# Cross-attention and expert layer on one core: the PV products of a quad in three bursts of two key tiles in place of two bursts of three

## The chip, the cores and the metric

One core of a Trainium2 chip runs the whole program. The metric is the device time of one execution in microseconds; the number compared is the median over runs. TensorE is PE in the profile (its weight loads PEld), VectorE DVE, ScalarE ACT, GpSimd POOL, SyncE SP.

## The reference

For 8 batch entries of 256 tokens and 128 channels there is a cross-attention with 16 heads of 8 dimensions. The keys and values of a head are 512 context rows, given, and the 256 own rows, projected from the layer-normalised input. A mixture of 8 experts, two for each token, follows.

```
qkv  = layernorm(x) @ w_qkv.T                    # q, own k, own v
k, v = concat(context k, k), concat(context v, v)   # 512 + 256 = 768 keys
attn = softmax(q * scale @ k.T)
x    = x + (attn @ v) @ w_proj.T + b_proj
x    = x + sum over the 2 chosen experts of weight * down(silu(gate(h)) * up(h)),   h = layernorm(x)
```

The change touches only `attn @ v`, and there only the order of the work.

## The kernel before, in words

Two functions run one after the other: `attend` (all of the attention) and `experts`. Each engine has its own instruction list, written out by hand; semaphores tie the lists together. Nothing plans or reorders the work.

`attend` handles the heads in quads of G = 4. There are QUADS = 32 of them: 8 batch entries times T = 4 quads. Quad q belongs to batch entry q // 4. The 768 keys are KT = 6 key tiles of 128. The program steps s from -2 to 33; b and r are s // 4 and s % 4. In step s three quads are in flight:

- Quad s + 2 has its row maxima computed. TensorE makes scores for that in six units (`max_half`, lines 528 and 533, each unit in two halves) into two PSUM buffers of two banks, `max_ps`. VectorE reduces each unit (`reduce_unit`, line 433). Half units wait until the unit two before has been reduced.
- Quad s has its scores made again, transposed and with the maximum already subtracted, in 12 units (`exp_unit`, line 550; unit 2k + a is key tile k and head pair a) into two single banks, `exp_ps[a]`. ScalarE exponentiates each unit into `probs` (line 392). Unit u waits until ScalarE has finished unit u - 2.
- Quad s - 1, and quad s itself, have their probabilities multiplied with the values: `pv_tile(q, k)` (line 560) is key tile k of quad q, four matmuls of 128 keys by 32 columns, one for each head, all accumulated into the one bank `pv_ps`. It waits for units 2k and 2k + 1 of ScalarE, and its first tile for the copy of the bank of the quad before.

TensorE's list in a step is GROUPS = 6 groups. Group i is: max half of one half of the rows, exp unit 2i, max half of the other half, exp unit 2i + 1. They are ordered so that neighbours use different halves of the array's rows. Between the groups stand other matmuls on whole rows: before group 1 the output projection of the batch entry before (r = 1, line 580) or the key and query projection (r = 2, lines 510 and 511); before group 3 the transposed maxima of the next quad (line 541); before group 4 the transposed result of quad s - 1 (line 568); before group 5 the transposed attention (r = 0, line 574), the transposed input (r = 1, line 505) or the value projection (r = 2, line 516). Those at r = 1 and 2 stop near the end of the batch. After group 1 and after group 4 stand the bursts of `pv_tile`s that the change moves.

ScalarE's list in a step is the 12 units, with the copy of `pv_ps` to SBUF (line 381) ahead of unit 4, which waits for the last `pv_tile` of quad s - 1, and the copy of the transposed maxima (line 386) ahead of unit 6. VectorE's list is the six reductions, with the normalising of quad s - 1 (lines 447 and 451, which wait for the transposed result) behind the fourth, and the merged row maxima (line 440) at the end. GpSimd refills the value columns of a quad when its products are done (`fill_values`, line 270). SyncE's queue spreads the keys and queries of quad s + 4 once all scores of quad s have been made.

Of the kernel before, what the change touches and what calls it, by code (L numbers as in the profile page):

```python
# [34 lines left out]
KT = CT + QT  # L35
# [14 lines left out]
def wait_for(engine, sem, value):  # L50

    if not isinstance(value, int) or value > 0:
        engine.wait_ge(sem, value)
# [39 lines left out]
def attend(nc, m, d):  # L93
# [13 lines left out]
    with ExitStack() as ctx:  # L107
# [55 lines left out]
        has_scores = lambda s: 0 <= s < QUADS  # L163
# [337 lines left out]
        def _(pe):  # L501
            def transpose_x(c):
                pe.wait_ge(norm_out, QT * (c + 1))
                for q in range(QT):
                    mm = pe.transpose(shared_ps[:, q * P:(q + 1) * P], xn[:, QT * c + q, :], m.ident[:])
                mm.then_inc(xt_filled, 1)

            def project_keys_queries(c):
                pe.wait_ge(xt_copied, c + 1)
                pe.matmul(shared_ps[:, 0:N], wqkv[:, C:2 * C], xnT[:], start=True, stop=True)  # L510
                pe.matmul(shared_ps[:, N:2 * N], wqkv[:, 0:C], xnT[:], start=True, stop=True).then_inc(kq_filled, 1)

            def project_values(c):
                pe.wait_ge(kq_copied, 2 * c + 2)
                for q in range(QT):
                    mm = pe.matmul(shared_ps[:, q * C:(q + 1) * C], xnT[:, q * P:(q + 1) * P], wqkv[:, 2 * C:3 * C],
                                   start=True, stop=True)
                mm.then_inc(v_filled, 1)

            def max_half(q, w, a):  # L520
                t, rows = q % T, slice(TILE * a, TILE * (a + 1))
                if w == 0 and a:
                    pe.wait_ge(rows_in[t], rows_spread(q))
                if a:
                    wait_for(pe, max_done, q * MUNITS + w - 1)
                if w < G:
                    g, i = divmod(w, QT)
                    mm = pe.matmul(max_ps[w % 2][:, a * BANK:(a + 1) * BANK], blocks[rows, t, g, i * P:(i + 1) * P],  # L528
                                   keys[rows, t, 0:NC_], start=True, stop=True)
                else:  # L530
                    for i in range(QT):
                        first = a * BANK + i * N
                        mm = pe.matmul(max_ps[w % 2][:, first:first + N], blocks[rows, t, w - G, i * P:(i + 1) * P],  # L533
                                       keys[rows, t, NC_:KEYS], start=True, stop=True)
                if a == 0:
                    mm.then_inc(max_filled, 1)

            def transpose_maxima(q):
                pe.wait_ge(split_max, 2 * q + 2)
                for i in range(QT):  # L540
                    mm = pe.transpose(shared_r[:, i * P:(i + 1) * P], maxes[:, q % 2, i, :], ident_r[:])
                mm.then_inc(maxT_filled, 1)

            def exp_unit(q, u):
                t, (k, a) = q % T, divmod(u, 2)
                rows = slice(TILE * a, TILE * (a + 1))
                if u == 0:
                    pe.wait_ge(max_in[t], 16 * (q // T + 1))
                wait_for(pe, exp_done, q * XUNITS + u - 1)
                pe.matmul(exp_ps[a][:], keys[rows, t, k * P:(k + 1) * P], blocks[rows, t], start=True, stop=True)\  # L550
                  .then_inc(exp_filled, 1)

            def pv_tile(q, k):
                t = q % T
                if k == 0:
                    pe.wait_ge(values_ready, 2 * q + 2)
                    wait_for(pe, pv_copied, q)
                pe.wait_ge(exp_done, q * XUNITS + 2 * (k + 1))
                for g in range(G):
                    mm = pe.matmul(pv_ps[ROWS * g:ROWS * (g + 1), 0:N], value_cols[:, t, k, g, :],  # L560
                                   probs[q % 2][:, k, g, :], start=(k == 0), stop=(k == KT - 1))
                if k == KT - 1:
                    mm.then_inc(pv_filled, 1)

            def transpose_out(q):
                pe.wait_ge(pv_copied, q + 1)
                for i in range(QT):
                    mm = pe.transpose(shared_ps[:, i * P:(i + 1) * P], pv_sb[:, i * P:(i + 1) * P], m.ident[:])
                mm.then_inc(out_filled, 1)

            def transpose_attention(b):
                pe.wait_ge(out_done, T * (b + 1))
                for i in range(QT):
                    mm = pe.transpose(shared_ps[:, i * P:(i + 1) * P], attn[:, i, :], m.ident[:])
                mm.then_inc(attnT_filled, 1)

            def project_out(b):
                pe.wait_ge(attnT_copied, b + 1)
                for i in range(QT):
                    mm = pe.matmul(shared_ps[:, i * C:(i + 1) * C], attnT[:, i, :], wproj[:], start=True, stop=True)  # L580
                mm.then_inc(proj_filled, 1)
# [13 lines left out]
            def step(s, b, r):  # L595
                for i in range(GROUPS):
                    if i == 1:
                        if r == 1 and b >= 1:
                            project_out(b - 1)
                        if r == 2 and b + 2 < B:  # L600
                            project_keys_queries(b + 2)
                    if i == 3 and has_scores(s + 1):
                        wait_for(pe, out_done, s - 1)
                        if r == 1 and b >= 1:
                            pe.wait_ge(proj_done, b)
                        if r == 2 and b + 2 < B:
                            pe.wait_ge(kq_copied, 2 * (b + 2) + 2)
                        if r == 3 and b + 2 < B:
                            pe.wait_ge(v_copied, b + 3)
                        transpose_maxima(s + 1)  # L610
                    if i == 4 and 1 <= s <= QUADS:
                        if has_scores(s + 1):
                            pe.wait_ge(maxT_copied, s + 2)
                        else:
                            wait_for(pe, out_done, s - 1)
                        transpose_out(s - 1)
                    if i == 5:
                        if r == 0 and b >= 1:
                            transpose_attention(b - 1)
                        if r == 1 and 0 <= b < B - 2:  # L620
                            pe.wait_ge(out_done, s)
                            transpose_x(b + 2)
                        if r == 2 and b + 2 < B:
                            wait_for(pe, out_done, s)
                            project_values(b + 2)
                    for a in range(2):
                        if has_scores(s + 2):
                            max_half(s + 2, i, 1 - a)
                        if has_scores(s):
                            exp_unit(s, 2 * i + a)  # L630
                    if i == 1 and has_scores(s - 1):
                        for k in range(KT // 2, KT):
                            pv_tile(s - 1, k)
                    if i == 4 and has_scores(s):
                        for k in range(KT // 2):
                            pv_tile(s, k)

            steps(step)


# [488 lines left out]
```

## Time and profile before

| | us |
|---|---|
| median of 3 runs (lowest, highest) | 576.71 (576.43, 577.19) |
| time of the profiled execution | 573.06 |
| its span | 571.5 |
| PE busy | 486.9 (85%) |
| DVE busy | 354.5 (62%) |
| ACT busy | 293.8 (51%) |
| POOL busy | 180.5 (32%) |

The span is that of the instructions in the profiled execution. An engine is busy while an instruction of its kind runs; matmuls are pipelined, so PE busy counts overlapping ones once and does not mean PE at its peak. In the chain that ended last only 2% of the span is named by an engine's line. The attention takes the first 363 us or so, the experts the rest.

### The profile page before, as it was taken

To read this page: it belongs to the slowest core of one execution; us is meant where nothing else is said; L and a number is where in the kernel's file an instruction comes from. 1 tells how busy PE (TensorE), PEld (TensorE's weight loads), DVE (VectorE), ACT (ScalarE), POOL (GpSimd) and SP (SyncE) were. 2 spreads that over 40 slices of the span, in tenths; PEclk is the share of its full clock that TensorE was granted. 3 is DMA by queue.
4 is the path that set the end of the run, shared out by engine and by line. 5 is a ranking of instruction groups with operands and counts; after the bars stand their busy time and mean duration, and the time that the engine had idled before them with its cause. 6 is when DMAs were issued, how large, how long until landed. Compare 5 with 4: busy or idle time off the path is not lost. (4 is left out here: it accounts for less than half of the span.)

```text
span 571.5 us, 10587 instructions
## 1 busy us (share of the span) xinstructions
PE 486.9 (85%) x3467; PEld 288.2 (50%) x3468; DVE 354.5 (62%) x646; ACT 293.8 (51%) x584; POOL 180.5 (32%) x381
## 2 busy tenths in 40 slices
PE   2689999999999999999999998465489999999940
PEld 1344555555555555555555543254346666676630
DVE  7696787787787787877787750547623333343316
ACT  1236776767678676767777775221023333333310
POOL 6141231312402311312300000103327766676630
PEclk9999999999999999999999997755589999999995
DMA  6502223233233333322122100340101111111126
GB/s 170 130 28 55 66 80 95 70 95 106 75 103 82 86 96 90 90 75 60 49 55 54 38 1 2 101 121 0 11 17 44 38 45 37 37 41 41 42 58 183
DMA packets 32254, 38.10 MB, mean 67 GB/s; under 512 B 5604, under 2 KB 20580, under 8 KB 32212
## 3 DMA queue, kind: packets, MB, share of 16 engines
q1 hardware_dynamic: 27252, 30.79, 20.0%
q0 software_dynamic: 2560, 5.25, 3.6%
q10 hardware_dynamic: 2400, 1.51, 0.9%
q8 instruction: 26, 0.43, 0.3%
q14 instruction: 16, 0.13, 0.1%
HBM read 16.58 MB, written 4.72 MB: 37 GB/s over the span
## 5 line engine op out<-in xcount | busy, mean ns | idle before, releaser
L433 DVE TENSOR_REDUCE max_part<-max_ps 128x2 f32<-128x1024 f32 (+1 forms) x192 | 231.8, 1222 | 69.1 <-PE max_ps L533 35.7
L392 ACT ACTIVATE probs<-exp_ps 128x512 f32<-128x512 f32 x384 | 207.3, 591 | 73.3 <-PE exp_ps L550 70.8
L550 PE MATMUL exp_ps<-blocks,keys 64*128 64x512 f32 x384 | 164.6, 483 | 12.6 <-ACT probs L392 12.6
L528 PE MATMUL max_ps<-keys,blocks 64*128 64x512 f32 x256 | 104.0, 458 | 6.7 <-DMA blocks<-masked 4.0
L560 PE MATMUL pv_ps<-probs,value_cols 128*32 128x256 f32 x1536 | 100.0, 394 | 0.2 <-ACT probs L392 0.2
L550 PEld LDWEIGHTS exp_ps<-blocks,keys 64*128 64x128 f32 x384 | 68.1, 187 | 49.2 <-issue 25.4
L995 DVE TENSOR_TENSOR hidden<-up_ps,silu 128x512 f32<-128x512 f32 x40 | 27.7, 692 | 82.0 <-PE up_ps L1085 79.8
L560 PEld LDWEIGHTS pv_ps<-probs,value_cols 128*32 128x32 f32 x1536 | 44.2, 112 | 40.5 <-issue 18.5
L309 POOL CAST maxes<-rowmax 128x8 fp32r<-128x8 f32 x32 | 6.3, 197 | 181.5 <-DVE rowmax L440 181.5
L528 PEld LDWEIGHTS max_ps<-keys,blocks 64*128 64x128 f32 x256 | 44.4, 195 | 30.6 <-DVE max_part L433 19.8
L888 ACT ACTIVATE hiddenT<-at_ps 128x512 f32<-128x512 f32 x40 | 23.9, 597 | 68.4 <-PE at_ps L1102 68.4
L533 PE MATMUL max_ps<-keys,blocks 64*128 64x256 f32 x256 | 48.1, 318 | 1.0 <-DVE max_part L433 1.0
L884 ACT ACTIVATE silu<-gate_ps 128x512 f32<-128x512 f32 x40 | 23.9, 597 | 43.0 <-PE gate_ps L1082 43.0
L1094 PEld LDWEIGHTS t_ps<-down,hiddenT 128*128 128x128 f32 x320 | 38.9, 192 | 14.0 <-issue 14.0
L1082 PE MATMUL gate_ps<-gate,xT 128*128 x80 | 43.4, 625 | 2.8 <-DVE xT L987 2.1
L832 POOL DMA_INDIRECT x_in<-h_rows,source_now x40 | 39.4, 986 | 17.2 <-issue 16.6
L1094 PE MATMUL t_ps<-down,hiddenT 128*128 x320 | 42.7, 276 | 2.4 <-ACT hiddenT L888 1.5
L856 POOL DMA_INDIRECT pick_outs<-y_out,target_now x40 | 39.5, 988 | 12.5 <-issue 9.2
L1085 PE MATMUL up_ps<-up,xT 128*128 x80 | 41.7, 604 | 0.0
L533 PEld LDWEIGHTS max_ps<-keys,blocks 64*128 64x128 f32 x256 | 31.9, 195 | 17.0 <-issue 8.1
L270 POOL COPY value_cols<-ctx_v_sb 128x128 f32<-128x128 f32 x32 | 9.7, 304 | 70.0 <-PE pv_ps L560 49.8
L1085 PEld LDWEIGHTS up_ps<-up,xT 128*128 128x128 f32 x80 | 15.5, 194 | 19.7 <-issue 19.7
(148 smaller groups left out, 465.0 us busy)
## 6 DMA issues: line engine op xcount, KB each, us to landing
keys<-parts SPq DMA_DIRECT2D x96, 96.0 KB
blocks<-masked SPq DMA_DIRECT2D x93, 64.0 KB
ctx_v_sb<-ctx_v_dram SPq DMA_DIRECT2D x8, 256.0 KB, 2.9
gate<-gateT_dram SPq DMA_DIRECT2D x8, 256.0 KB, 2.7
up<-upT_dram SPq DMA_DIRECT2D x8, 256.0 KB, 2.9
y_in<-pick_outs SPq DMA_DIRECT2D x8, 256.0 KB, 4.5
raw<-ctx_kT_dram SPq DMA_DIRECT2D x7, 256.0 KB, 2.6
h_rows<-h SPq DMA_DIRECT2D x4, 256.0 KB, 4.9
```

The lines of the kernel that those rows point to most:

```text
L392: act.activation(probs[par][:, k, PAIR * a:PAIR * (a + 1)], exp_ps[a][:].rearrange("p (g n) -> p g n", n=N), ACT.Exp).then_inc(exp_done, 1)
L433: vec.reduce_max(out, bank, axis=AX.X).then_inc(max_done, 1)
L528: mm = pe.matmul(max_ps[w % 2][:, a * BANK:(a + 1) * BANK], blocks[rows, t, g, i * P:(i + 1) * P], keys[rows, t, 0:NC_], start=True, stop= ...
L533: mm = pe.matmul(max_ps[w % 2][:, first:first + N], blocks[rows, t, w - G, i * P:(i + 1) * P], keys[rows, t, NC_:KEYS], start=True, stop=True)
L550: pe.matmul(exp_ps[a][:], keys[rows, t, k * P:(k + 1) * P], blocks[rows, t], start=True, stop=True)\
L560: mm = pe.matmul(pv_ps[ROWS * g:ROWS * (g + 1), 0:N], value_cols[:, t, k, g, :], probs[q % 2][:, k, g, :], start=(k == 0), stop=(k == KT - 1))
L832: pool.indirect_dma_start(x_in[:, r, :], None, h_dram, bass.IndirectOffsetOnAxis(ap=source_now[:, r:r + 1], axis=0))\
L856: pool.indirect_dma_start(outs_dram, bass.IndirectOffsetOnAxis(ap=target_now[:, before2:before2 + 1], axis=0), y_out[:, before2, :], None) ...
L995: vec.tensor_tensor(hidden[:, r % 2, :], up_ps[r % 2][:], silu[:, r % 2, :], ALU.mult)\
L1082: pe.matmul(gate_ps[r % 2][:], xT[:, r % 2, :], m.gate[:, bass.ds(e, 1), :].rearrange("p a i -> p (a i)"), start=True, stop=True).then_inc ...
L1085: pe.matmul(up_ps[r % 2][:], xT[:, r % 2, :], m.up[:, bass.ds(e, 1), :].rearrange("p a i -> p (a i)"), start=True, stop=True).then_inc(up_ ...
L1094: mm = pe.matmul(y_ps[:, 0:C], hiddenT[:, r % 2, c, :], down[:, bass.ds(e, 1), c, :].rearrange("p a h -> p (a h)"), start=(c == 0), stop=( ...
```

## The change

The first burst of a quad is now two key tiles behind group 3, the second two behind group 5, the third the last two behind group 1 of the next step.

```diff
                     if i == 1 and has_scores(s - 1):
-                        for k in range(KT // 2, KT):
+                        for k in (4, 5):
                             pv_tile(s - 1, k)
-                    if i == 4 and has_scores(s):
-                        for k in range(KT // 2):
+                    if i in (3, 5) and has_scores(s):
+                        for k in (i - 3, i - 2):
                             pv_tile(s, k)
```

The number of matmuls and their operands are the same. No wait is added or taken away in `pv_tile`.

## Rows read from the trace of the kernel before

**Rows 1.** Busy time by stretch: PE, PEld, DVE, ACT, POOL, clock, DMA share, GB/s.
```profile
210.00:240.00 30.00, 29.02 (x252) 15.90 (x250) 23.02 (x28) 22.08 (x47) 8.97 (x19) 1.00 0.33 87
...
330.00:362.00 32.00, 27.25 (x214) 12.03 (x206) 7.28 (x15) 19.49 (x40) 0.41 (x2) 0.89 0.01 1
```

**Rows 2.** Waits in the whole span: us in total, times, longest.
```profile
ACT probs L392 <- PE exp_ps L550: 70.8, 94, 3.8
...
PE exp_ps L550 <- ACT probs L392: 12.6, 35, 0.8
```

**Rows 3.** Timeline of PE, step s = 19 (r = 3): start, us, what.
```profile
228.52 0.47 PE L550 MATMUL exp_ps<-blocks,keys 64*128 64x512 f32 x1 [0.33 <-ACT probs L392]
...
230.22 0.50 PE L550 MATMUL exp_ps<-blocks,keys 64*128 64x512 f32 x1
...
230.64 1.50 PE L560 MATMUL pv_ps<-probs,value_cols 128*32 128x256 f32 x24
...
232.08 0.72 PE L550 MATMUL exp_ps<-blocks,keys 64*128 64x512 f32 x2
...
233.27 0.49 PE L550 MATMUL exp_ps<-blocks,keys 64*128 64x512 f32 x1
...
234.18 0.44 PE L568 MATMUL shared_ps<-ident,pv_sb 128*128 128x128 f32 x2
...
234.55 0.49 PE L550 MATMUL exp_ps<-blocks,keys 64*128 64x512 f32 x1
...
236.82 0.49 PE L550 MATMUL exp_ps<-blocks,keys 64*128 64x512 f32 x1
...
237.16 0.39 PE L550 MATMUL exp_ps<-blocks,keys 64*128 64x512 f32 x1
...
237.38 0.38 PE L528 MATMUL max_ps<-keys,blocks 64*128 64x512 f32 x1
...
238.10 0.47 PE L550 MATMUL exp_ps<-blocks,keys 64*128 64x512 f32 x1 [0.34 <-ACT probs L392]
```

**Rows 4.** Timeline of ACT and DVE in the same step.
```profile
232.21 0.39 ACT L381 ACTIVATE pv_sb<-pv_ps 128x256 f32<-128x256 f32 x1 [0.86 <-PE pv_ps L560]
...
232.62 1.09 ACT L392 ACTIVATE probs<-exp_ps 128x512 f32<-128x512 f32 x2
...
235.55 1.21 DVE L433 TENSOR_REDUCE max_part<-max_ps 128x4 f32<-128x1024 f32 x1
...
237.36 1.08 ACT L392 ACTIVATE probs<-exp_ps 128x512 f32<-128x512 f32 x2 [1.19 <-PE exp_ps L550]
```

**Rows 5.** Timeline of PE, steps s = 17 (r = 1) and s = 18 (r = 2).
```profile
207.91 0.46 PE L550 MATMUL exp_ps<-blocks,keys 64*128 64x512 f32 x1 [0.33 <-ACT probs L392]
...
217.88 0.47 PE L550 MATMUL exp_ps<-blocks,keys 64*128 64x512 f32 x1 [0.32 <-ACT probs L392]
...
218.69 0.70 PE L510 MATMUL shared_ps<-xnT,wqkv 128*128 128x256 f32 x2
...
220.42 1.50 PE L560 MATMUL pv_ps<-probs,value_cols 128*32 128x256 f32 x24
...
226.59 0.71 PE L516 MATMUL shared_ps<-wqkv,xnT 128*128 128x128 f32 x4
227.23 0.38 PE L533 MATMUL max_ps<-keys,blocks 64*128 64x256 f32 x1
```

**Rows 6.** Timeline of PEld and PE behind the last maxima, steps 30 and 31.
```profile
343.91 0.20 PEld L560 LDWEIGHTS pv_ps<-probs,value_cols 128*32 128x32 f32 x4 [0.23 <-ACT probs L392]
344.34 0.20 PEld L560 LDWEIGHTS pv_ps<-probs,value_cols 128*32 128x32 f32 x4 [0.23 <-issue]
...
349.77 2.62 PE L560 MATMUL pv_ps<-probs,value_cols 128*32 128x256 f32 x24
```

**Rows 7.** Weight loads around a PV burst of step 19: start, us, idle before.
```profile
230.64 1.02 PEld L560 LDWEIGHTS pv_ps<-probs,value_cols 128*32 128x32 f32 x24 [0.25 <-issue]
...
232.07 0.18 PEld L528 LDWEIGHTS max_ps<-keys,blocks 64*128 64x128 f32 x1 [0.41 <-DVE max_part L433]
```

## The prediction

> **What bounds the kernel now.** I read first the busy time by stretch. From 210 to 240 us PE is busy 29.02 of 30 us at a granted clock of 1.00, DVE 23.02, ACT 22.08; that is the steady part of the attention, and the change lies wholly in it [rows 1]. So PE's list sets the pace. But a busy PE holds short stalls, so I read the waits next: ACT waits 70.8 us in total for PE's scores, and PE 12.6 us for ACT [rows 2]. Each waits for the other in turn, which points to a two-buffer loop that bursts tear open. The timeline of one step shows it. Step 19 runs from the first exp unit at 228.52 to that of step 20 at 238.10, 9.58 us. Between unit 8 (234.55) and unit 10 (236.82) PE has the second burst of three tiles, and no score reaches ACT before 237.36: it sat idle 1.19 us. PE is through with group 5 at 237.38, but unit 0 of the next step starts at 238.10, as ACT has only just begun on unit 10, whose bank it needs [rows 3, 4].
>
> **The rules of the walk**, all from that step. An exp unit that starts on PE starts on ACT 0.54 later (236.82, 237.36). Two units on ACT take 1.09, one 0.59, so they follow at 0.50. When ACT ends a unit, PE starts the next one for its bank 0.06 later (232.62 + 0.59 = 233.21, PE at 233.27); at unit 0 it is 0.15 (237.36 + 0.59 = 237.95, PE at 238.10). From an odd exp unit to a burst or a whole-row matmul it is 0.42 (230.22 to 230.64), to another score matmul only 0.22 (237.16 to 237.38). A burst of three takes 1.44 to the next work (230.64 to 232.08), two transposes 0.37 (234.18 to 234.55) [rows 3, 4].
>
> **A burst of two.** A tile is two passes of four matmuls (24 records for three tiles). In a slow stretch the weight loads of passes follow at 0.43 (343.91, 344.34) at half clock, so a pass is 0.213 at full clock and three tiles 1.28 of the 1.44: the fixed part is 0.15. Two tiles: 0.15 + 0.85 = 1.00. Ends: 0.96 if there were no fixed part (two thirds of 1.44), and 1.44 - 0.43 + 0.31 = 1.32 if the gap of the weight loads around a burst, 0.25 + 0.41 = 0.66 [rows 7], were all fixed and not 0.35 of it as in the walk (0.20 of entry, 0.15). I take 1.00, as the pass is a direct row. Three bursts come to 3.00, against 2.88 for two [rows 3, 6].
>
> **The steady step after, from unit 0 at time 0.**
> Unit 0 ends on ACT at 1.13, unit 1 at 1.63, so unit 3 starts at 1.69 and the burst at 2.11. Before it is 230.64 - 228.52 = 2.12: nothing gained, since ACT's chain sets this part and covers the smoother PE. The burst ends at 3.11 (-0.44). From there to the end of group 3 the copy of pv_ps, units 4 and 5 and the maxima copy on ACT set the time, as before: 234.18 - 232.08 = 2.10, to 5.21. The copy of pv_ps is long done, so the burst placed here waits for nothing: its tiles 0 and 1 need units 0 to 3. It ends at 6.21, the two transposes at 6.58, where unit 8 starts. Before, unit 8 came at 234.55, 0.37 behind the same point; it is 1.00 later now. Units 8 and 9 reach ACT at 7.12 and 7.62. With no burst behind group 4, unit 10 waits for unit 8: 7.12 + 0.59 + 0.06 = 7.77; unit 11 comes 0.50 later at 8.27. This is a new stall: PE would be free at 6.58 + 0.58 (a group of line 533, 236.81 to 237.38) = 7.16. The last burst starts at 8.69 and ends at 9.69, and by then ACT has done units 10 and 11 (8.31 + 1.09 = 9.40), so the stall ahead of unit 0 is gone [rows 3, 4].
>
> - r = 3: 9.69 against 9.58, +0.11.
> - r = 0 and r = 1: the two whole-row matmuls before group 5 have the shape of the transposes of 0.37 and fit into the new stall (7.16 + 0.20 for the change to whole rows + 0.37 = 7.73, under 7.77), and the output projection before group 1 at r = 1, of the four records of the value projection (227.23 - 226.59 = 0.64), fits into the first one (0.22 + 0.42 + 0.64 = 1.28; unit 3 waits until 1.69 all the same). So 9.69 against 217.88 - 207.91 = 9.97: -0.28 [rows 5].
> - r = 2: the projections before group 1 are longer. Before, 220.42 - 217.88 = 2.54 up to the burst; now unit 1 starts 0.22 behind unit 0 and the projections at 0.64 in place of 0.81, so 2.37. The value projection then sets group 5: unit 8 at 6.84, unit 9 0.34 later, +0.42, +0.64 gives 8.24 for unit 10, +0.34 +0.42 +1.00 gives 10.00 against 228.52 - 217.88 = 10.64: -0.64 [rows 3, 5].
>
> Of steps 1 to 29, 13 are of the -0.28 kind (7 at r = 0, 6 at r = 1), 6 of the -0.64 kind, 10 of the +0.11 kind (7 at r = 3, and the late ones that have no matmuls before group 5). Sum: -3.6 - 3.8 + 1.1 = -6.3.
>
> **Edges.** Steps 0 and 30: +0.11 each. In step 31 the burst behind group 3 puts 1.00 in front, the one of 1.44 behind group 4 goes, and units 10 and 11 wait some 0.9 for ACT, with the last tiles right behind unit 11 either way: +0.5, an estimate by the same rules. Together +0.7. At the end the granted clock drops for a while, 0.89 over the stretch from 330 to 362, and the burst at 349.77 takes 2.62 in place of 1.50 [rows 1, 3, 6]. There are three such bursts (one in step 0, two at the end), so some 3.4 us. I take this as unchanged, and keep -3 and +3 for it. VectorE: the normalising of quad s - 1 now waits for the transposes, until about 6.7, and takes under 0.5; the fifth reduction has its scores at about 7.4, takes 1.21 and ends at 8.6; its buffer is wanted at 9.69, a slack of 1.1 [rows 4]. SP's spread of the next rows starts right behind unit 11, now about 0.9 ahead of the next unit 0 (9.69 - 8.27 - 0.49) and 0.5 before; the spread of the maxima to unit 0 has both new bursts between, in place of one. None is late. POOL's refill is released 0.44 earlier. The experts, which use other code, are untouched.
>
> Sum: -6.3 + 0.7 = -5.6. The profiled time would go from 573.06 to 567.5. The median of the runs lies 3.65 above that execution; by the same difference 576.71 becomes 571.1.
>
> A rule speaks against the change. Going from scores to a burst costs 0.20 more than from scores to scores (0.42 against 0.22), and a burst has 0.15 of fixed time [rows 3]. The Trainium skill, TensorEngine Tiling (Array Packing), Key Properties, says that changing the tiling mode, not just the tile, drains the engine. By that rule, the trace agrees, and there are one or two such changes more in a step; the walk has them by rows.
>
> **Rivals.**
> 1. *The drains cost more than the walk has* (slower). Mechanism: at each entry and exit of a burst PE stands empty. For it: the weight loads show 0.66 of gap per burst, not 0.35 [rows 7]. Against it: whatever hides in 1.44 is measured for three tiles, so only the pass could be mis-sized. The two old bursts hold their gap already, so of the price of 1.32 the one added burst pays 0.31 x 32 = 9.9: 571.1 + 9.9 = 581.0. It decides from 5.6 / 32 = 0.18 a step. Chance 0.09.
> 2. *ACT's loop takes it all back* (no change). If units 10 and 11 each come 0.15 and not 0.06 behind ACT's end, 0.2 a step is added in the 26 steps that hang on that chain (23 steady ones, three at the edges): 5.2 us, 576.3. For it: 0.15 stands at unit 0. Against it: 0.06 stands at unit 6. Chance 0.15.
> 3. *More than the walk*: the half-clock bursts vanish (-3.4) and a burst costs 0.96 (3 x 0.04 x 32 = -3.8): 563.9. Chance 0.08.
> 4. *The forecast*, 568.5 to 573.5. Chance 0.68.
>
> **How the numbers follow.** The measurement tells 0.2%, 1.15 us, from no change. Faster is the forecast and rival 3, 0.76; same is rival 2, 0.15; slower is rival 1, 0.09. The range 565 to 577 takes in the forecast, rival 2 and the near part of rival 3.
>
> **What would show it.** In a steady step three bursts of 1.00 each; r = 0 and 1 steps of 9.7, r = 2 of 10.0, r = 3 of 9.7, where three kinds of step have become alike; no wait of unit 0 for ACT, but one of unit 10 in its place; ACT's idle of 1.2 us behind the burst gone. It is wrong if the bursts take 1.2 or more, if the steady step is not shorter at r = 2, or if DVE's reductions stand in the waits of PE.

## The result, and the profile after

| | before | changed |
|---|---|---|
| median of all runs (lowest, highest), us | 576.95 (576.43, 578.33), 4 runs | 567.23 (566.46, 570.91), 4 runs |
| time of the profiled execution | 573.06 | 566.54 |
| its span | 571.5 | 565.0 |
| PE busy | 486.9 | 482.2 |
| DVE busy | 354.5 | 363.3 |
| ACT busy | 293.8 | 293.7 |

The ratio is 0.987, with a 95% interval of 0.982 to 0.991. Timed again in five more rounds it was 0.984, 0.979 to 0.990; one execution of the kernel before, 686.02 us at a mean granted clock of 0.638, is left out of that ratio. The change makes the kernel faster, by 1.3% and by 1.6% in the two timings.

The steady part, by the view that the prediction began with [rows 1]:

```profile
210.00:240.00 30.00, 29.18 (x259) 15.58 (x252) 24.62 (x30) 21.97 (x47) 8.33 (x18) 1.00 0.33 87
```

The columns are busy time of PE, PEld, DVE, ACT and POOL, the clock, the DMA share and GB/s. DVE is busy 24.62 of 30 us, before 23.02. Only part of this is a quicker pace: from 60 to 300 us its busy time rises from 187.07 to 196.98 us, of which the reductions (line 433) make 3.2. Most of the rest is overlap that is gone: the records of its instructions overlapped for 6.9 us in that window before, now for 0.9. The waits of the whole span, which answer to [rows 2]:

```profile
ACT probs L392 <- PE exp_ps L550: 70.9, 86, 3.8
...
DVE rsum L447 <- PE shared_ps L568: 31.8, 32, 9.3
...
PE exp_ps L550 <- ACT probs L392: 11.1, 33, 0.7
```

The sum of ACT's waits is the same, 70.9 and 70.8, and so nearly is PE's. These two sums over the whole span would have said that nothing happened. The timeline says where the waits now are. These are lines of PE's list from unit 0 of step 19 at 223.92 to unit 0 of step 20 at 233.67, and they answer to [rows 3]:

```profile
223.92 0.72 PE L550 MATMUL exp_ps<-blocks,keys 64*128 64x512 f32 x2
...
225.16 0.49 PE L550 MATMUL exp_ps<-blocks,keys 64*128 64x512 f32 x1 [0.29 <-ACT probs L392]
...
225.65 0.50 PE L550 MATMUL exp_ps<-blocks,keys 64*128 64x512 f32 x1
226.08 1.07 PE L560 MATMUL pv_ps<-probs,value_cols 128*32 128x256 f32 x16
...
227.09 0.72 PE L550 MATMUL exp_ps<-blocks,keys 64*128 64x512 f32 x2
...
229.18 1.07 PE L560 MATMUL pv_ps<-probs,value_cols 128*32 128x256 f32 x16
230.19 0.44 PE L568 MATMUL shared_ps<-ident,pv_sb 128*128 128x128 f32 x2
...
230.56 0.50 PE L550 MATMUL exp_ps<-blocks,keys 64*128 64x512 f32 x1
...
231.75 0.50 PE L550 MATMUL exp_ps<-blocks,keys 64*128 64x512 f32 x1 [0.23 <-ACT probs L392]
...
232.66 1.07 PE L560 MATMUL pv_ps<-probs,value_cols 128*32 128x256 f32 x16
233.66 0.49 PE L528 MATMUL max_ps<-keys,blocks 64*128 64x512 f32 x1
233.67 0.72 PE L550 MATMUL exp_ps<-blocks,keys 64*128 64x512 f32 x2
```

Unit 0 and unit 1 of step 20 (233.67) now start right behind the third burst, with no wait in between: the stall of unit 0 is gone. A burst of two takes 226.08 to 227.09, 1.01. Units 2 and 10 wait for ACT. The idle time of ACT is not gone either, it has moved. This is unit 8 on ACT in the same step:

```profile
231.09 1.09 ACT L392 ACTIVATE probs<-exp_ps 128x512 f32<-128x512 f32 x2 [1.19 <-PE exp_ps L550]
```

Before, the 1.19 us stood ahead of unit 10 [rows 4]. What the new order changes is where PE pays for it. PE no longer stands still ahead of unit 0, and in its new wait ahead of unit 10 the whole-row matmuls that stand before group 5 at r = 0 and r = 1 find room.

I measure the kernel in three parts by the starts of the transposed results (line 568), one in each step: steps 1 to 29 (the 28 distances between those starts), the last three distances, and the rest.

| us | before | changed | difference |
|---|---|---|---|
| start to the transposes of step 1 | 52.98 | 52.79 | -0.2 |
| steps 1 to 29 | 279.61 | 275.26 | -4.35 |
| last three | 27.66 | 24.46 | -3.2 |
| from there to the end of the span | 211.25 | 212.49 | +1.2 |
| span | 571.5 | 565.0 | -6.5 |

So the gain has two parts of similar size, and the second was not in the forecast. The last difference is within what one kernel shows by itself: from the last transposes to the end took 209.8 to 214.0 us in all eleven traces of this study, 211.3 and 214.0 in the two of the kernel before. These two windows, of the kernel before and then of the changed one, show its cause, the granted clock in the column before the DMA share:

```profile
336.00:352.00 16.00, 13.67 (x92) 0.83 0.01 2
```

```profile
336.00:352.00 16.00, 13.12 (x118) 1.00 0.01 2
```

The changed kernel runs its last two steps at 2.4 GHz throughout. The kernel before fell to 1.2 GHz in two stretches. A burst of three takes 1.50 in its steady steps; it took 2.62 us in the second stretch [rows 6], and in the first one:

```profile
343.49 2.79 PE L560 MATMUL pv_ps<-probs,value_cols 128*32 128x256 f32 x24
```

### The profile page after: what moved, and what is told of

It is laid out like the page before. It is cut to its first block and busy times, and to the rows that moved or that the text cites. A ratio compares the mean times of both kernels' runs of the same rounds, so it can differ in the third digit from the quotient of the medians.

```text
span 565.0 us, 10587 instructions
## 1 busy us (share of the span) xinstructions
PE 482.2 (85%) x3467; PEld 284.5 (50%) x3468; DVE 363.3 (64%) x646; ACT 293.7 (52%) x584; POOL 180.8 (32%) x381
## 5 line engine op out<-in xcount | busy, mean ns | idle before, releaser
L392 ACT ACTIVATE probs<-exp_ps 128x512 f32<-128x512 f32 x384 | 208.0, 593 | 75.7 <-PE exp_ps L550 70.9
L550 PE MATMUL exp_ps<-blocks,keys 64*128 64x512 f32 x384 | 161.4, 475 | 11.1 <-ACT probs L392 11.1
L528 PE MATMUL max_ps<-keys,blocks 64*128 64x512 f32 x256 | 98.4, 464 | 6.8 <-DMA blocks<-masked 4.1
L560 PE MATMUL pv_ps<-probs,value_cols 128*32 128x256 f32 x1536 | 103.1, 386 | 0.0
L550 PEld LDWEIGHTS exp_ps<-blocks,keys 64*128 64x128 f32 x384 | 65.2, 186 | 38.0 <-ACT probs L392 34.6
L995 DVE TENSOR_TENSOR hidden<-up_ps,silu 128x512 f32<-128x512 f32 x40 | 27.7, 692 | 83.3 <-PE up_ps L1085 81.1
L560 PEld LDWEIGHTS pv_ps<-probs,value_cols 128*32 128x32 f32 x1536 | 40.4, 109 | 41.1 <-issue 24.4
L447 DVE RECIPROCAL rsum<-shared_ps 128x8 f32<-128x8 f32 x32 | 6.7, 208 | 31.8 <-PE shared_ps L568 31.8
```

What stands on the lines that cost most here:

```text
L392: act.activation(probs[par][:, k, PAIR * a:PAIR * (a + 1)], exp_ps[a][:].rearrange("p (g n) -> p g n", n=N), ACT.Exp).then_inc(exp_done, 1)
L995: vec.tensor_tensor(hidden[:, r % 2, :], up_ps[r % 2][:], silu[:, r % 2, :], ALU.mult)\
```

## The experiments

### Which part of the gain is where

steady_only has the new bursts for quads 0 to 29 and the old ones for 30 and 31; tail_only is its mirror. The edit of steady_only, against the changed kernel:

```diff
-                    if i == 1 and has_scores(s - 1):
-                        for k in (4, 5):
+                    if has_scores(s - 1):
+                        for k in ({1: (4, 5)} if s - 1 < 30 else {1: (3, 4, 5)}).get(i, ()):
                             pv_tile(s - 1, k)
-                    if i in (3, 5) and has_scores(s):
-                        for k in (i - 3, i - 2):
+                    if has_scores(s):
+                        for k in ({3: (0, 1), 5: (2, 3)} if s < 30 else {4: (0, 1, 2)}).get(i, ()):
                             pv_tile(s, k)
```

> Three bursts of two for quads 0 to 29, the old two bursts of three for quads 30 and 31. In the kernel as changed the transposed results of step 1 to 29 came 4.4 us closer together than before, those of the last three 3.2 us, where the granted clock stayed 1.00 in place of falling. Theory (the gain is of two kinds, stalls in the steady steps and the half-clock bursts at the end): about 4.4 us under the kernel before, with the half-clock bursts back in the last two steps. Rival (the clock at the end depends on the steady steps before it): 7.5 us under. Rival (the steady steps give nothing beyond the end): 0 to 1 us under.

> The mirror of steady_only: two bursts of three for quads 0 to 29, three of two for quads 30 and 31. Theory: the steady steps as before (9.58 to 10.64 us), and about 3 us under the kernel before from a granted clock that stays at 1.00 behind the last maxima. Rival (the clock at the end has another cause): within 0.5 us of before, with a burst there still at 2.6 us or more.

steady_only: 569.13 us, ratio to before 0.986 (0.977 to 0.995). tail_only: 571.76 us, ratio 0.992 (0.988 to 0.997). The timings can't part the theories, since the executions of one kernel differ by more than the effect that parts them: the kernel before took 573.05 to 581.59 us beside these two. The traces can. Steps 1 to 29 took 275.30 in steady_only and 279.33 in tail_only; the last three 27.14 and 25.30 (one step of them, where the orders meet, has a burst of two more in tail_only and one less in steady_only: 10.57 and 8.74). Each part of the gain comes with its own part of the edit. Bursts at the end of steady_only and then of tail_only:

```profile
338.08 1.50 PE L560 MATMUL pv_ps<-probs,value_cols 128*32 128x256 f32 x24
...
349.06 2.79 PE L560 MATMUL pv_ps<-probs,value_cols 128*32 128x256 f32 x24
352.50 2.19 PE L560 MATMUL pv_ps<-probs,value_cols 128*32 128x256 f32 x24
```

```profile
345.27 1.07 PE L560 MATMUL pv_ps<-probs,value_cols 128*32 128x256 f32 x16
348.43 1.07 PE L560 MATMUL pv_ps<-probs,value_cols 128*32 128x256 f32 x16
351.53 1.07 PE L560 MATMUL pv_ps<-probs,value_cols 128*32 128x256 f32 x16
355.00 1.93 PE L560 MATMUL pv_ps<-probs,value_cols 128*32 128x256 f32 x32
```

A burst of three is 1.50 at full clock and 2.79 at half clock. None of tail_only's bursts of two is slow.

### Does the end repeat

Both kernels were run again without an edit.

> The kernel before, unchanged, for a second trace. Question: is the half clock behind the last maxima a property of the order of work or of the single execution? Theory (order of work): steps 1 to 29 at 279.6 us, the last three at 27.7, with bursts of 2.6 us or more, as in the first trace. Rival (chance of the execution): the last three anywhere from 24.5 to 31 us, steps 1 to 29 the same.

> The changed kernel, unchanged, timed in five more rounds and traced again. Theory (the gain is 4.4 us in the steady steps and some 3 us at the end, both of them properties of the order): steps 1 to 29 at 275.3 us, the last three at 24.5 with a clock of 1.00; ratio 0.983 to 0.988. Rival (the end is chance): the steady part the same, the last three anywhere up to 28 us, ratio nearer to 0.992.

before_again took 579.22 us in its one execution; after_again 565.02 (563.74 to 570.11), ratio 0.984 (0.979 to 0.990). Steps 1 to 29 repeat to 0.3 us: 279.36 and 275.18. The last three repeat in the changed kernel, 24.46 again. In the kernel before they do not: 32.21 in place of 27.66. Its clock in the same window:

```profile
336.00:352.00 16.00, 14.32 (x82) 0.56 0.01 2
```

So the order and the single execution both have a share. That the old order falls to half clock at the end showed in all three traces that have it there (27.66, 32.21, and steady_only's 27.14); how much it falls differs from one execution to the next. The new order held 1.00 in the window of all its three traces, and of kq_early's below. That is a likely reason why the medians differ by more (9.7 and 8.7 us) than the first two profiled spans (6.5): the first trace of before was one of the mild cases, with 573.06 us against a median of 576.95. That it explains all of the difference was not shown.

### Size of a burst against its place

threes_late and threes_early have two bursts of three, like the kernel before, with the one of tiles 0 to 2 behind group 5 or group 3 in place of 4. The difference from the kernel before:

```diff
-                    if i == 4 and has_scores(s):
+                    if i == 5 and has_scores(s):        # threes_early: i == 3
                         for k in range(KT // 2):
                             pv_tile(s, k)
```

> Two bursts of three as before, but tiles 0 to 2 behind group 5 in place of group 4. Theory (what counts is that ACT has work from both banks when a burst starts and that no wait stands behind it, not the size of the burst): the stall of unit 0 goes, one of unit 10 comes; steps of 9.58 at r = 3 (no change), 9.58 at r = 0 and 1 (before 9.97), 9.9 at r = 2 (before 10.64); 9 us under the kernel before in the steady steps, so about 567. Rival (short bursts are what gives the gain): no gain, since ACT drains behind each burst of three as before, 576 or more.

> Two bursts of three, tiles 0 to 2 behind group 3 (before: group 4; threes_late: group 5, which took the steps to 9.6 to 9.95 us). Theory (placement decides which stall is left; at group 3 the burst ends ahead of the whole-row matmuls, and unit 10 waits for ACT, which covers them): steps of 9.5 at r = 3, 9.5 at r = 0 and 1, about 10.5 at r = 2, where the long value projection isn't covered; 6 to 7 us less than before over steps 1 to 29. Rival (a burst that stands late in the step is what gave threes_late its gain, by giving ACT work before unit 0): no gain or a loss, since unit 0 still waits for ACT.

threes_late: 571.24 us, ratio 0.988 (0.979 to 0.996). Steps 1 to 29 took 273.31, which is 6.3 less than before and 2.0 less than the changed kernel. So the number and size of the bursts are not what gives the steady gain of the change: the same two bursts of three, one group later, give more. Expected were 9 us less than before. Steps of the r = 3 kind came out (9.61, expected 9.58). At r = 0 and 1 a step took 9.69 and 9.67 (expected 9.58), at r = 2 10.17 (expected 9.9). What the walk missed there is a wait before group 5; this is one at r = 0:

```profile
202.07 0.44 PE L574 MATMUL shared_ps<-ident,attn 128*128 128x128 f32 x2 [0.25 <-DVE attn L451]
```

With no burst behind group 4 TensorE reaches these transposes before VectorE has normalised quad s - 1. The last three steps took 31.08, much of them at half clock: 3.4 us more than in the first trace of before and 1.1 less than in the second, so this part of the difference can't be put down to the order.

threes_early: 585.17 us, ratio 1.014 (1.009 to 1.020), slower. My expectation of 9.5 us a step was an error of addition: it set out from 5.21, the end of group 3 behind a first burst of two, where with a burst of three it is 2.12 + 1.44 + 2.10 = 5.66. Done right the rules give 5.66 + 1.44 + 0.37 + 1.19 (unit 8 to 10) + 1.27 (unit 10 to unit 0) = 9.93, and the trace shows 9.93 to 9.95 in undisturbed steps at r = 0, 1 and 3. So the rival written beside it holds: there is a loss, and unit 0 waits for ACT as before. That is the smaller part of it. Steps 1 to 29 took 286.0 us, 6.4 more than before, and 4.5 of this is the clock: in three of the steady steps, which took 11.4 us each in place of 9.94, it fell. The order itself costs some 1.9 us there. The last three steps took 31.84 (27.66 and 32.21 before). This is one of the three steady steps, in windows of 2 us:

```profile
312.00:314.00 2.00, 2.00 (x9) 1.24 (x8) 1.97 (x4) 1.69 (x4) 0.00 (x0) 1.00 0.00 0
314.00:316.00 2.00, 2.00 (x12) 0.88 (x16) 1.81 (x2) 1.72 (x4) 0.41 (x2) 0.65 0.63 155
316.00:318.00 2.00, 2.00 (x24) 0.71 (x16) 0.53 (x1) 0.20 (x1) 0.00 (x0) 0.50 0.36 95
318.00:320.00 2.00, 2.00 (x14) 1.18 (x10) 1.10 (x1) 1.72 (x5) 0.47 (x2) 1.00 0.00 0
```

### The price of one burst more

six_ones has a tile behind each of the six groups. The edit, against the changed kernel:

```diff
-                    if i == 1 and has_scores(s - 1):
-                        for k in (4, 5):
+                    if has_scores(s - 1):
+                        for k in {0: (4,), 1: (5,)}.get(i, ()):
                             pv_tile(s - 1, k)
-                    if i in (3, 5) and has_scores(s):
-                        for k in (i - 3, i - 2):
+                    if has_scores(s):
+                        for k in {2: (0,), 3: (1,), 4: (2,), 5: (3,)}.get(i, ()):
                             pv_tile(s, k)
```

> One key tile behind each of the six groups: tiles 0 to 3 behind groups 2 to 5, tiles 4 and 5 behind groups 0 and 1 of the next step. Theory (a burst of n tiles costs 0.15 + 0.43 n, entering it 0.20, and what bounds a group is ACT's two-buffer loop, which a tile behind each group covers): a burst of one takes 0.58; by the rules of the walk a step at r = 3 takes 8.5 us, unless VectorE, which has 7.9 to 8.5 us of work in a step, sets it; so 8.5 to 9.2 a step, 545 to 560 us for the kernel. Rival (each entry and exit drains the array at a price that the bursts of three and two hid): a burst of one takes 0.8 or more, steps of 10 us or more, slower than before.

549.23 us, ratio 0.951 (0.943 to 0.959): 28 us less than before. Steps 1 to 29 took 260.21 us, the last three 21.41. From unit 0 to unit 0 a step takes 8.75 at r = 0, 9.50 at r = 1 and 8.63 at r = 3 (8.54 in the late steps that have none of the extra matmuls), where the walk had 8.5 for r = 3. At r = 2 it takes 10.64, as in the kernel before: there six bursts gain nothing. PE's list around groups 2 to 4 of step 16:

```profile
190.71 0.72 PE L550 MATMUL exp_ps<-blocks,keys 64*128 64x512 f32 x2
191.05 0.39 PE L528 MATMUL max_ps<-keys,blocks 64*128 64x512 f32 x1
191.37 0.64 PE L560 MATMUL pv_ps<-probs,value_cols 128*32 128x256 f32 x8
191.94 0.37 PE L541 MATMUL shared_ps<-ident_r,maxes 128*128 128x128 f32 x2
192.24 0.50 PE L528 MATMUL max_ps<-keys,blocks 64*128 64x512 f32 x1
192.24 0.49 PE L550 MATMUL exp_ps<-blocks,keys 64*128 64x512 f32 x1
...
192.90 0.64 PE L560 MATMUL pv_ps<-probs,value_cols 128*32 128x256 f32 x8
193.47 0.44 PE L568 MATMUL shared_ps<-ident,pv_sb 128*128 128x128 f32 x2
```

A burst of one takes 191.37 to 191.94, 0.57. With 1.01 for two and 1.44 for three that is a straight line, 0.14 + 0.43 n. So an added burst costs 0.14 and what entering it costs. The walk had 0.20 for the latter, and in these groups even that does not show: the burst starts 0.32 behind the last score matmul (191.05, 191.37), and where scores follow scores it is 0.34 (190.71, 191.05). A burst as dear as the rival that made the kernel slower had it, 0.8 for one tile, is out. No unit waits for ACT in these groups, and the profile shows no idle time of PE in them: it works where it used to wait.

### A queue of copies at r = 2

kq_early is the changed kernel, and six_kq is six_ones, each with this edit in ScalarE's list:

```diff
-                    if u == 4:
+                    if u == 2:
                         if r == 2 and b + 2 < B:
                             copy_keys_queries(b + 2)
+                    if u == 4:
                         if 1 <= s <= QUADS:
```

> The changed kernel, with ScalarE's two copies of the projected keys and queries ahead of unit 2 in place of unit 4 (r = 2 only). In the changed kernel the step at r = 2 took 10.13 us from unit 0 to unit 0, where the walk of the prediction had 10.00: these copies end 0.4 us behind the short burst, and the copy of pv_ps and unit 4 queue behind them. Theory: they now lie in ACT's idle time ahead of unit 2, the step falls to 9.95 to 10.0, six steps, 0.9 us in all. Rival (the step is set elsewhere): 10.13 as before.

> six_ones with the same move of the two copies. There the step at r = 2 has PE waiting 0.39 us at tile 0 for the copy of pv_ps, which stands behind them. Theory: this wait goes, 6 x 0.4 to 0.6 = 2.4 to 3.6 us under six_ones, about 546. Rival (the time is taken elsewhere, by VectorE or the projections): within 0.5 us of six_ones, 549.

The changed kernel's ACT in step 18, from the two copies of lines 347 and 348 to unit 4:

```profile
217.03 0.39 ACT L347 ACTIVATE raw<-shared_ps 128x256 f32<-128x256 f32 x1
217.29 0.40 ACT L348 ACTIVATE raw<-shared_ps 128x256 f32<-128x256 f32 x1
217.56 0.42 ACT L381 ACTIVATE pv_sb<-pv_ps 128x256 f32<-128x256 f32 x1
217.82 0.64 ACT L392 ACTIVATE probs<-exp_ps 128x512 f32<-128x512 f32 x1
```

PE ended the burst before them at 217.18, and the copy of pv_ps began 0.38 later; in step 19 it began 0.13 behind it. In kq_early the step at r = 2 takes 9.98 or 9.99 in place of 10.12, and steps 1 to 29 take 274.38, 0.88 less; 564.94 us, ratio 0.980 (0.975 to 0.986). In six_kq the step takes 10.30 in place of 10.64 and steps 1 to 29 take 258.15, 2.06 less than six_ones; 545.06 us, ratio 0.946 (0.941 to 0.951). The 2.06 is a little under the 2.4 to 3.6 expected; the medians of six_ones and six_kq lie 4.2 apart, but they were not timed beside each other. six_kq is the fastest kernel of this study. Its steady part:

```profile
60.00:300.00 240.00, 240.00 (x2184) 118.97 (x2184) 207.30 (x251) 193.28 (x395) 59.80 (x145) 1.00 0.32 85
```

The profile shows PE busy in all of the 240 us; in the kernel before it was 232.11. That is no proof that nothing waits, since the ends of matmuls are modelled. In the same window weight loads still wait 2.7 us for ACT in 14 places and some 7 us for VectorE's normalising in 17, most of it hidden behind matmuls already under way. But the loops between PE and ACT have little left to give.

## Why the prediction was right, and where its terms were off

The forecast was 571.1 us, 5.6 us less; the medians gave 567.2 and 565.0, which is 9.7 and 8.7 less, and the profiled execution 6.5 less. Direction and the mechanism of the steady steps hold. That the number came as near as it did is luck in part: the steady steps gave 2 us less than forecast, and the end, where the forecast had a loss, gave 3 us. The step from the profiled execution to the median was off too. It carried over the 3.65 us by which the kernel before lay above its profiled execution; for the changed kernel that distance was 0.7 and 0.5 us.

**What bounds the kernel.** Right. PE paces the steady steps by stalls that the busy share hides. threes_late, threes_early and six_ones show it by moving only the bursts. One sign that was named did not come: the 1.2 us of ACT's idle time did not go, it moved from unit 10 to unit 8. The walk itself has it so, with unit 8 1.00 later and nothing for ACT to do before it.

**The rules of the walk.** They came out one by one in step 19. From unit 0 to the first burst 2.16 (2.11 forecast), the burst 1.01 (1.00), to the second 2.10 (2.10), that burst 1.01, transposes 0.37 (0.37), unit 8 to unit 10 1.19 (1.19). The steps at r = 0, 1 and 3 take 9.75, against 9.69. They have become alike, as forecast. The +0.11 for r = 3 was +0.17, the -0.28 for r = 0 and 1 -0.21. Most of the missing 0.06 lies ahead of the first burst: unit 0 starts on ACT 0.59 behind its start on PE (223.92, 224.51), where the rule had 0.54 for every unit.

**The r = 2 step**: -0.64 was -0.52, 10.12 in place of 10.00. The step that failed is "From there to the end of group 3 ... as before: 2.10": two more ScalarE copies stand in that queue at r = 2, and the long burst had covered them. kq_early shows it: with these two copies moved the step takes 9.99.

**The steady sum**: -6.3 was -4.35; three traces with the old order there lie at 279.3 to 279.6 us, three with the new one at 275.2 to 275.3. By kinds 13 x -0.21 + 6 x -0.52 + 10 x +0.17 = -4.15, from unit 0 to unit 0.

**The edges**: +0.7 was -3.4 (-0.2 at the start, -3.2 at the end). What follows the last transposes, the experts above all, was taken as untouched. It took 1.2 us more in this pair of traces and 3.4 less in the second pair, so it shows no effect of the change. The prediction saw the half-clock bursts, named -3 as one end and took them as unchanged. tail_only and steady_only show that the order of the last two steps decides whether they fall. Which part of the order does was not tried on its own, but the eleven traces sort by the size of the bursts: with bursts of three at the end, at any of the three places, the clock fell in all five, and with bursts of two or one tile it held 1.00 to the last transposes in all six.

**The slower rival**, drains at 0.66 a burst, is out: one, two and three tiles lie on a line with 0.14 at its foot. The gap of weight loads around a burst is no idle time of PE in the profile: the score matmuls' records run on until the burst's first (225.65 + 0.50 reaches beyond 226.08). The 0.20 of entry that the walk took from step 19 is at most a bound, as six_ones shows. **The rival of no change** saw units 10 and 11 at 0.15 behind ACT's end; unit 10 was 0.07 behind it (ACT began unit 8 at 231.09 and took 0.59; PE started at 231.75). **The rival of more** had its clock half right and its burst half wrong.

**VectorE** was forecast not to be late. It isn't. It now waits for the transposes in each step, as the walk had it: 31.8 us in 32 times, where before it was 22.4 us in 3 long waits; from 60 to 300 us it is 10.0 us in 25 times, and none before. In the steady steps of the changed kernel that holds up nobody. In threes_late it does.

## What to carry to other kernels

When TensorE feeds two-buffer loops on other engines, place its independent bulk work in pieces about as long as the loop's wait, one behind each group, and count a fixed price for each piece; here it was 0.14 us and up to 0.20 on entry, against stalls of 0.3 to 0.7. Where the bulk stands matters as well as how large its pieces are: the same burst of three cost 1.4% one group earlier and gained 1.2% one group later, though the clock has a share in both (over the steady steps 1.9 us more without the clock's part, and 6.3 less). A walk of one step by five or six rules read from a timeline was good to 0.1 us in most steps and missed by 0.3 at the worst, where another engine's queue came into play; each kind of step needs its own list of what is queued on every engine.

## What was not expected of the hardware

The granted clock fell to 1.2 GHz in the midst of stretches in which PE shows no idle time (in threes_early 2.00 of 2.00 us busy from 312 to 318, with the clock at 1.00, then 0.65, then 0.50), so busy PE in such a view does not tell that the clock is safe. At the end of the attention it fell in every trace with bursts of three there, though PE was busy for longer in them (13.67 and 14.32 of 16 us in the two of the kernel before, 13.12 in the changed one), and by different amounts in two executions of the same program: 27.7 and 32.2 us for the same three steps.
